# Products without a reader in TensorE's gaps, a new order for the first batch, and rows turned by DMA, in a cross-attention and quantised FFN kernel

## The chip, the core and the metric

The kernel runs on one core of one Trainium2 chip. The metric is the device time of one execution in microseconds; the kernel before was executed three times, and one further execution was recorded by the hardware profiler. All times below come from that recording and those runs. TensorE works at one of two clocks, 1.2 or 2.4 GHz; the profile gives the granted clock as a share of the higher one.

## The reference

Eight batches of 512 x 512 rows in float32. First an attention whose keys and values are the same context, then a feed-forward layer whose inputs, weights and hidden block are rounded to 8-bit steps:

```python
# x, context: (8, 512, 512); mask: (8, 512, 512) bool, True is masked
q = layernorm(x)
s = where(mask, -1e9, einsum('bqd,bkd->bqk', q, context) / sqrt(512))
att = einsum('bqk,bkd->bqd', softmax(s), context)
x = x + einsum('bdl,ol->bdo', swapaxes(att, -1, -2), W_merge) + b_merge

xq = fake_quant(layernorm(x), clip_x)      # one scale: the largest |value| of all batches
g  = xq @ weight_quant(w_gate).T           # w_gate, w_up: (1408, 512)
u  = xq @ weight_quant(w_up).T
h  = fake_quant(silu(g) * u, clip_down)    # again one scale for all batches
x  = x + h @ weight_quant(w_down).T        # w_down: (512, 1408)
```

Both scales need a maximum over all batches. So the kernel has three parts, one after the other: attention for all batches, gate and up for all batches, down for all batches.

## The kernel before

**Attention** (`attention`, from line 86). A batch of 512 rows is T = 4 tiles of 128. Products are made in three float32 pieces: each operand is split into a high part (copied by ScalarE) and a low part (subtracted by VectorE), and `product` (L744) adds hi·hi, hi·lo and lo·hi, over four steps of contraction twelve matmuls of 128x512 into one PSUM bank. For a batch, TensorE turns the context (turns g = 0 to 3, four 128x128 transposes each) and the normalised rows (turns g = 4 to 7) by `transposes` (L726) into the banks `tr[g % 4]`; ScalarE copies the high part out (`transposed_hi`, L367) and VectorE subtracts the low part (`transposed_lo`, L480). Then come the scores (`scores`, banks mm0 to mm3), the mask and row maximum on VectorE (`mask_and_max`, L527), the exponential on ScalarE, the sum's inverse, `probs_hi` and `probs_lo` (L544), the products with W_merge (`mixed`, L769), and those with the context (`merged`, L762), to which VectorE adds the residual. The order of work is written out by hand for each engine; the engines meet only by semaphores. From the second batch on the products of batch n - 1, the turns of batch n + 1 and the scores of batch n are woven together.

The first batch has an order of its own. Its rows and its context come in four DMAs each; SP issues row tile 0, context tiles 0 to 3, row tiles 1 to 3, the mask, W_merge, and then the loads of the next batch (L261 to L273). TensorE turns the four context tiles and then, for k = 0 to 3, row tile k, scores(0,k), and a quarter of W_merge (`merge_transpose`, L776, into `tr[k]`). VectorE takes the row statistics of tile t (`first_norm`, L493), POOL raises the variance to the power -1/2 (`make_rstd1`, L319), VectorE makes the bias (`first_bias`, L502). Only when all four tiles are through does POOL turn the mask into a summand, in one piece of 128x2048 (`make_mneg`, L313). VectorE then goes through the tiles one at a time: mask and maximum, a low part of W_merge (`merge_lo`, L487), the inverse, and `probs_lo` of the same tile, which waits for ScalarE's exponential and `probs_hi`. The turns of batch 1's context wait for the low parts of W_merge, since they share banks; `mixed(0, 0)` waits for all of them (L773).

SP also stores the finished rows, and turns the quantised weights by DMA transposes (`turn_w`, L238: L242 turns a tile of 128x512 float16, L246 one of 128x1408).

At its end attention leaves two last steps to VectorE and POOL: the variances of the last batch's rows, and the largest distance from the mean.

**Gate and up** (`ffn`, from line 813). The largest value of all rows is found by a turn on TensorE (L1181), a reduction, a second turn (L1183) and a few small operations of VectorE. Then the rows of batch 0 are scaled and rounded to int8 (`layer_norm` on ScalarE, L979, half of batch 0 by VectorE, L1087), cast to float16 integers `xi` (`quantise`, L1057), turned by TensorE in 16 transposes of 128x128 (`turn`, L1153, banks tp0 and tp1), and copied out to `xT` (`take_xT`, L985, and L1093). A step is one batch: for each of NI = 11 tiles `gate_up` (L1168) makes four matmuls for gate and four for up, ScalarE takes silu (L996), VectorE multiplies (L1074) and keeps the largest (L1082). The next batch is scaled at i = 0 of the step, cast at i = 2 and 3, turned by TensorE behind i = 6 and copied out by ScalarE behind i = 8:

```python
                    def step(b, p):
                        for i in range(NI):
                            gate_up(b, p, i)
                            if i == 6 and not static(b, B - 1):
                                turn(b + 1, 1 - p)
```

Five hidden blocks stay in SBUF; the first three of the eight are stored to DRAM by SP (L932, 2.8 MB each) after their step, and SP loads the rows of batch n + 2 (L920) when those of batch n have been scaled.

**Down.** The maximum over all hidden values is found by POOL (L963). ScalarE rounds each hidden block in four pieces (L1022), VectorE casts them (`widen_hidden`, L1118), and TensorE makes 44 matmuls per batch (`down`, L1194, L1210); VectorE scales and adds the residual, SP stores.

## Time and profile before

| | |
|---|---|
| three runs | 579.19, 579.25, 579.32 us; median 579.25 |
| the profiled execution | 579.35 us, its span 577.6 us |
| TensorE | 543.1 us busy, 94% of the span, 2610 matmuls; mean granted clock 0.976 |
| VectorE, ScalarE, POOL | 454.3, 296.1 and 148.8 us busy |
| DMA | 82.59 MB, 143 GB/s over the span; 306 GB/s in the first of 40 slices |
| attention, first batch to the products with W_merge | 0 to 41.6 us |
| attention, to its last product | 41.6 to 318.7 us |
| from there to gate/up's first product | 318.7 to 329.8 us |
| gate and up, eight steps | 329.8 to 490.5 us |
| from there to down's first product | 490.5 to 495.5 us |
| down, to its last product | 495.5 to 573.1 us |

A line of the profile names the line of the kernel, the engine, the operation, and what it writes and reads; a duration is that of one instruction as recorded. Matmuls are pipelined, so the recorded durations overlap, and the pace is the distance between starts. In `ffn` several names share one tile: `xi`, `xT` and silu's results appear as `hid`, the float16 hidden block as `gu_T`, and four of the output banks as `gu`, two as `tp`.

### The profile page before, as it was taken

What the parts mean: (1) busy time and instruction counts of PE and PEld (TensorE: products, weight loads), DVE (VectorE), ACT (ScalarE), POOL (GpSimd) and SP (SyncE); (2) the same over time, 40 slices, a digit from 0 to 9 for tenths busy, and PEclk for the clock granted to TensorE, in tenths of its full rate; (3) what the DMA queues carried; (4) which work ended last, traced back from release to release, by engine and by line L of the source; (5) the groups of instructions that cost most, each with busy time, mean ns of one, the idle gap of its engine ahead of it and who ended that gap; (6) DMA issues with size and microseconds to landing.
All of it is one profiled execution on the core that took longest, in us unless ns stands there. A gap on an engine that the chain in (4) does not pass through costs nothing. (4 is left out here: it accounts for less than half of the span.)

```text
span 577.6 us, 7625 instructions
## 1 busy us (share of the span) xinstructions
PE 543.1 (94%) x2610; PEld 359.9 (62%) x2610; DVE 454.3 (79%) x839; ACT 296.1 (51%) x431; POOL 148.8 (26%) x77
## 2 busy tenths in 40 slices
PE   6759999999999999999999499999999999699996
PEld 4547888888888888888888244444444444244442
DVE  5279889887988988889686557878777877599884
ACT  3356465545645556355431357556645743777520
POOL 1707454636545365463421000000000000000000
PEclk9969999999999999999999699999999999899999
DMA  8520535454354443441229513272060000779783
GB/s 306 184 74 1 133 136 183 136 189 88 119 174 128 170 124 121 165 134 74 48 112 150 186 73 170 104 273 73 12 260 0 0 0 2 269 269 396 244 288 153
DMA packets 47583, 82.59 MB, mean 143 GB/s; under 512 B 20416, under 2 KB 24512, under 8 KB 44992
## 3 DMA queue, kind: packets, MB, share of 16 engines
q1 hardware_dynamic: 47552, 82.20, 42.8%
q8 instruction: 17, 0.28, 0.2%
q14 instruction: 14, 0.11, 0.1%
HBM read 52.43 MB, written 25.43 MB: 135 GB/s over the span
## 5 line engine op out<-in xcount | busy, mean ns | idle before, releaser
L1176 PE MATMUL gu<-hid,gu_T 128*128 128x512 f16 x704 | 155.6, 383 | 0.8 <-DVE hid L1093 0.8
L1176 PEld LDWEIGHTS gu<-hid,gu_T 128*128 128x128 f16 x704 | 68.9, 99 | 84.1 <-issue 3.3
L1074 DVE SCALAR_TENSOR_TENSOR hid<-gu,gu_mul,hid 128x512 f32 (+1 forms) x88 | 65.2, 747 | 41.0 <-PE gu L1176 35.7
L996 ACT ACTIVATE hid<-gu,gu_mul 128x512 f32<-128x512 f32 x88 | 59.8, 686 | 70.4 <-PE gu L1176 64.9
L1210 PE MATMUL gu<-wd_T,gu_T 128*128 128x512 f16 x264 | 59.1, 385 | 5.0 <-DVE gu_T L1118 5.0
L546 DVE SCALAR_TENSOR_TENSOR p_lo<-probs,rinv,p_hi 128x512 fp32r<-128x512 f32 x32 | 39.8, 1243 | 21.4 <-ACT p_hi L386 21.0
L750 PE MATMUL mm<-cT_hi,qT_hi 128*128 128x512 f32 x128 | 51.2, 400 | 5.6 <-DVE qT_lo L484 5.6
L1022 ACT ACTIVATE h<-hid,inv 128x512 int8<-128x512 f32 (+3 forms) x32 | 44.2, 1456 | 17.9 <-DVE gu_T L1118 14.1
L1082 DVE TENSOR_REDUCE hmax<-hid 128x1 f32 (+2 forms) x48 | 53.1, 1119 | 0.0
L750 PE MATMUL mm<-wm_hi,p_hi 128*128 128x512 f32 x128 | 53.0, 414 | 0.0
L379 ACT ACTIVATE probs<-probs,nmax 128x512 f32<-128x512 f32 x32 | 23.2, 724 | 56.7 <-DVE nmax L537 56.7
L750 PE MATMUL mm<-g_hi,c_hi 128*128 128x512 f32 x128 | 52.2, 408 | 0.0
L344 POOL TENSOR_TENSOR c_lo<-cx,c_hi 128x2048 fp32r<-128x2048 f32 x8 | 37.0, 4626 | 54.3 <-ACT c_hi L414 54.2
L752 PE MATMUL mm<-wm_hi,p_lo 128*128 128x512 f32 x128 | 50.7, 396 | 0.0
L752 PE MATMUL mm<-cT_hi,qT_lo 128*128 128x512 f32 x128 | 50.4, 394 | 0.0
L751 PE MATMUL mm<-wm_lo,p_hi 128*128 128x512 f32 x128 | 50.4, 394 | 0.0
L751 PE MATMUL mm<-cT_lo,qT_hi 128*128 128x512 f32 x128 | 50.4, 394 | 0.0
L752 PE MATMUL mm<-g_hi,c_lo 128*128 128x512 f32 x128 | 50.2, 393 | 0.0
L751 PE MATMUL mm<-g_lo,c_hi 128*128 128x512 f32 x128 | 49.9, 390 | 0.0
L1210 PEld LDWEIGHTS gu<-wd_T,gu_T 128*128 128x128 f16 x264 | 26.0, 99 | 37.5 <-DVE gu_T L1118 5.8
L963 POOL PARTITION_ALL_REDUCE top<-hmax x1 | 0.4, 380 | 171.2 <-DVE hmax L1106 171.2
L393 ACT ACTIVATE g_hi<-mm 128x512 fp32r<-128x512 f32 x32 | 19.0, 597 | 48.5 <-PE mm L752 48.5
(123 smaller groups left out, 958.6 us busy)
## 6 DMA issues: line engine op xcount, KB each, us to landing
h_dram<-hid SPq DMA_DIRECT2D x3, 2816.0 KB, 12.9
hid<-h_dram SPq DMA_DIRECT2D x3, 2816.0 KB, 14.0
cx<-in_ctx_dram SPq DMA_DIRECT2D x7, 1024.0 KB, 7.5
x<-in_x_dram SPq DMA_DIRECT2D x5, 1024.0 KB, 5.3
x_dram<-x SPq DMA_DIRECT2D x20, 256.0 KB, 2.4
xq<-x_dram SPq DMA_DIRECT2D x5, 1024.0 KB, 5.9
x<-x_dram SPq DMA_DIRECT2D x5, 1024.0 KB, 6.4
hid<-x_dram SPq DMA_DIRECT2D x4, 1024.0 KB, 6.5
```

The lines of the kernel that those rows point to most:

```text
L344: nc.gpsimd.tensor_tensor(c_lo[:], cx[n % 2][:], c_hi[:].bitcast(F32), ALU.subtract).then_inc(c_ready, 1)
L379: nc.scalar.activation(probs[t % 3][:], probs[t % 3][:], ACT.Exp, bias=nmax[:, t:t + 1], scale=SCALE, accum_out=rsum[:, t:t + 1]).then_inc ...
L546: nc.vector.scalar_tensor_tensor(p_lo[:, t, :], probs[t % 3][:], rinv[:, t:t + 1], p_hi[:, t, :].bitcast(F32), ALU.mult, ALU.subtract).the ...
L750: nc.tensor.matmul(bank[:], a_hi[:, t, cols], b_hi[:, t, :], start=t == 0, stop=False)
L751: nc.tensor.matmul(bank[:], a_hi[:, t, cols], b_lo[:, t, :], start=False, stop=False)
L752: last = nc.tensor.matmul(bank[:], a_lo[:, t, cols], b_hi[:, t, :], start=False, stop=t == T - 1)
L996: nc.scalar.activation(silu[SILU_AT[i]], gu[2 * (i % 3)][:], ACT.Silu, scale=gu_mul[:, 0, i:i + 1]).then_inc(silu_done, 1)
L1022: nc.scalar.activation(h8[:, a:b, :].rearrange("p i l -> p (i l)"), hid[:, slot2(s), a * L:b * L], ACT.Copy, scale=inv[:, 1:2]).then_inc(h ...
L1074: nc.vector.scalar_tensor_tensor(hid[:, b % SLOTS, i * L:(i + 1) * L], gu[2 * (i % 3) + 1][:], gu_mul[:, 1, i:i + 1], silu[SILU_AT[i]], AL ...
L1082: nc.vector.tensor_reduce(hmax[:, k:k + 1], hid[:, b % SLOTS, lo * L:hi * L], AX_X, ALU.max, apply_absolute_value=True).then_inc(hmaxed, 1)
L1176: last = nc.tensor.matmul(gu[2 * (i % 3) + g][:], gu_T[:, g, h, i * P:(i + 1) * P], xT[p][:, h, :], start=h == 0, stop=h == T - 1)
L1210: last = nc.tensor.matmul(yb[T * (s % 2) + t][:], hq[s % 2][:, i, t * P:(t + 1) * P], wd_T[:, i, :], start=i == 0, stop=i == NI - 1)
```

## The change

It has four parts.

1. *First batch.* TensorE's order of turns becomes context 0, rows 0, context 1, 2, 3 (`FIRST_TURNS`); the turns of row tiles 1 to 3 stand in the middle of scores(0,0), (0,1) and (0,2), and go to banks mm1, mm2, mm3 and tr0. The quarters of W_merge follow scores(0,0), (0,1) and, two together, (0,2), in banks tr1, tr2, tr3, tr1. Row tiles 2 and 3 share their statistics, their rstd and their bias. POOL makes the mask's summand in four pieces, the first ahead of the last rstd. VectorE makes `probs_lo` of tile t - 1 behind the mask of tile t; the row statistics of batch 1 come before its context's subtractions.
2. *Rows turned by DMA.* For batches 1 to 7 SP issues four DMA transposes from `xi` to `xT`; TensorE's turns, ScalarE's copies and their waits go. SP's order in a step becomes: load of the batch after next, wait for the casts, four transposes, then (batches 1 to 3) wait for the maximum and store of the hidden block of the batch before.
3. *Products without a reader.* 13 behind attention's last product, 11 ahead of the turns of batch 0, 4 behind them, and 20 between up and down.
4. Waits and counts of semaphores follow.

```diff
+                FIRST_TURNS = (0, T, 1, 2, 3, T + 1, T + 2, T + 3)
+                def turns(n, g):
+                    return 2 * T * n + (FIRST_TURNS.index(g) if n == 0 else g) + 1
+                def turn_bank(n, g):
+                    if n == 0 and T <= g < 2 * T - 1:
+                        return mm[g - T + 1]
+                    return tr[0] if n == 0 and g == 2 * T - 1 else tr[g % 4]
+                FIRST_ROWS = ((0, 1), (1, 2), (2, T))
+                def merge_bank(k):
+                    return tr[1 + k % 3]
...
# POOL
-                    make_rstd1(0)
-                    make_mneg(0)
+                    first_rstd(0)
+                    first_rstd(1)
+                    first_mneg(0)
+                    first_rstd(2)
+                    for t in range(1, T):
+                        first_mneg(t)
...
# ScalarE
-                    for g in range(T + 1):
+                    for g in FIRST_TURNS[:T + 1]:
                         transposed_hi(0, g)
                     norm1(0, 1)
+                    transposed_hi(0, T + 1)
                     norm1(0, 2)
-                    transposed_hi(0, T + 1)
                     norm1(0, 3)
-                    transposed_hi(0, T + 2)
...
                             exps(n, t)
                             if start:
-                                if t == 0:
-                                    transposed_hi(0, 2 * T - 1)
+                                if t < 2:
+                                    transposed_hi(0, T + 2 + t)
                                 probs_hi(n, t)
-                                merge_hi(t)
+                                for k in ((0,), (1,), (2, 3), ())[t]:
+                                    merge_hi(k)
...
# VectorE
-                    first_norm(0)
+                    first_stats(0)
                     first_bias(0)
...
-                    for g in range(T + 1):
+                    transposed_lo(0, 0)
+                    transposed_lo(0, T)
+                    first_stats(1)
+                    for g in (1, 2, 3):
                         transposed_lo(0, g)
-                    for t in range(1, T):
-                        first_norm(t)
-                        first_bias(t)
-                        if t > 1:
-                            transposed_lo(0, T + t - 1)
+                    first_bias(1)
+                    first_stats(2)
+                    first_bias(2)
+                    transposed_lo(0, T + 1)
...
                             if start:
-                                if t == 0:
-                                    transposed_lo(0, 2 * T - 1)
-                                else:
-                                    merge_lo(t - 1)
+                                if t:
+                                    probs_lo(n, t - 1)
+                                    for k in ((0,), (1,), (2, 3))[t - 1]:
+                                        merge_lo(k)
                                 invert_sum(n, t)
-                                probs_lo(n, t)
+                                if t < 2:
+                                    transposed_lo(0, T + 2 + t)
...
                         if start:
-                            merge_lo(T - 1)
-                            for k in range(T):
+                            probs_lo(n, T - 1)
+                            row_stats1(n + 1, 0, T)
+                            transposed_lo(n + 1, 0)
+                            row_bias1(n + 1)
+                            for k in range(1, T):
                                 transposed_lo(n + 1, k)
-                            row_stats1(n + 1, 0, T)
-                            row_bias1(n + 1)
...
# TensorE
                         for t in range(T):
+                            if turn is not None and t == T // 2:
+                                transposes(0, turn)
...
                     pe.wait_ge(consts, 4)
-                    for g in range(T):
+                    for g in FIRST_TURNS[:T + 1]:
                         transposes(0, g)
                     for n in range(B):
                         last, start = n == B - 1, n == 0
                         for k in range(T):
-                            if start:
-                                transposes(0, T + k)
                             scores(n, k)
                             if start:
-                                merge_transpose(k)
+                                for g in ((0,), (1,), (2, 3), ())[k]:
+                                    merge_transpose(g)
...
                     for k in range(T):
                         merged(B - 1, k)
+                    for _ in range(13):
+                        nc.tensor.matmul(tr[0][:], c_hi[:, 0, 0:P], g_hi[:, 0, :], start=True, stop=True)
...
# gate and up: SP
-                    for b in range(SPILL):
-                        for n in (2 * b, 2 * b + 1):
-                            sp.wait_ge(affine, T * (n + 1))
-                            if n == 0:
-                                sp.wait_ge(own_affine, T // 2)
+                    sp.wait_ge(affine, T)
+                    sp.wait_ge(own_affine, T // 2)
+                    load(2, 0, x_in)
+                    for n in range(1, B):
+                        sp.wait_ge(affine, T * (n + 1))
+                        if n + 2 < B:
                             load(n + 2, n % 2, x_in)
-                        sp.wait_ge(hrun, b + 1)
-                        sp.dma_start(h_dram[b], hid[:, b, :]).then_inc(slot_free, 16)
-                        sp.wait_ge(slot_free, 16 * (SLOTS + b + 1))
+                        sp.wait_ge(ints, 2 * (n + 1))
+                        for t in range(T):
+                            sp.dma_start_transpose(xT[n % 2][:, :, t * P:(t + 1) * P], xi[:, t, :]).then_inc(xT_in[n % 2], 16)
+                        if n <= SPILL:
+                            sp.wait_ge(hrun, n)
+                            if n > 1:
+                                sp.wait_ge(slot_free, 16 * (SLOTS + n - 1))
+                            sp.dma_start(h_dram[n - 1], hid[:, n - 1, :]).then_inc(slot_free, 16)
...
# gate and up: ScalarE, VectorE, TensorE
-                            if i == 8 and not last:
-                                take_xT(b + 1, 1 - p)
...
-                        if not static(b, 0):
-                            dve.wait_ge(turned, 2 * b)
+                        if static(b, 1):
+                            dve.wait_ge(turned, 2)
+                        elif not static(b, 0):
+                            dve.wait_ge(xT_in[1 - p], times(b, 2 - p, 64) - 64 * p)
...
                         if i == 0:
-                            pe.wait_ge(xT_out, 2 * (b + 1))
+                            if static(b, 0):
+                                pe.wait_ge(xT_out, 2)
+                            else:
+                                pe.wait_ge(xT_in[p], times(b, p, 64) - 64 * (1 - p))
...
+                    def keep_busy(products, bank):
+                        for _ in range(products):
+                            nc.tensor.matmul(bank[:], wd_T[:, 0, 0:P], wd_T[:, 1, :], start=True, stop=True)
...
+                    keep_busy(11, gu[5])
                     turn(0, 0)
+                    keep_busy(4, gu[5])
                     def step(b, p):
                         for i in range(NI):
                             gate_up(b, p, i)
-                            if i == 6 and not static(b, B - 1):
-                                turn(b + 1, 1 - p)
...
+                    keep_busy(20, tp[0])
                     for s in range(B):
                         down(s)
```

## Rows read from the trace of the kernel before

**Rows 1.** Waits of TensorE over the span: us in total, times, longest.
```profile
PE tr L740 <- DVE wm_lo L490: 6.6, 3, 2.8
PE mm L750 <- DVE qT_lo L484: 5.6, 4, 1.4
PE gu L1210 <- DVE gu_T L1118: 5.0, 1, 5.0
PE tp L1181 <- DVE tops L1042: 4.3, 1, 4.3
PE tp L1163 <- DVE hid L1067: 2.7, 1, 2.7
```

**Rows 2.** Timeline of TensorE, first batch: start us, us, line, operation, idle before.
```profile
4.14 4.00 PE L740 MATMUL tr<-ident,cx 128*128 128x128 f32 x16 [4.14 <-DMA cx<-in_ctx_dram]
...
10.41 0.80 PE L750 MATMUL mm<-cT_hi,qT_hi 128*128 128x512 f32 x1 [1.41 <-DVE qT_lo L484]
...
22.58 0.50 PE L750 MATMUL mm<-cT_hi,qT_hi 128*128 128x512 f32 x1 [1.41 <-DVE qT_lo L484]
...
25.45 0.60 PE L781 MATMUL tr<-ident,x 128*128 128x128 f32 x4
25.88 0.60 PE L740 MATMUL tr<-ident,qn 128*128 128x128 f32 x4
...
41.60 0.77 PE L750 MATMUL mm<-wm_hi,p_hi 128*128 128x512 f32 x1
```

**Rows 3.** Timelines of VectorE and POOL, first batch.
```profile
5.32 0.55 DVE L644 TENSOR_SCALAR qn<-xq,rstd,nmr 128x512 f32<-128x512 f32 x1
...
18.92 5.41 POOL L317 TENSOR_SCALAR mneg<-mk 128x2048 bf16<-128x2048 uint8 x1
...
29.88 0.68 DVE L533 CUSTOM_DVE_ANT_0 probs<-mm,mneg 128x512 f32<-128x512 f32 x1
...
32.59 0.75 DVE L546 SCALAR_TENSOR_TENSOR p_lo<-probs,rinv,p_hi 128x512 fp32r<-128x512 f32 x1 [0.79 <-ACT p_hi L386]
```

**Rows 4.** Busy time and granted clock in short windows (clock: third number from the end).
```profile
320.80:321.00 0.20, 0.00 (x0) 0.00 (x0) 0.17 (x3) 0.00 (x0) 0.00 (x0) 0.76 0.96 369
...
334.40:334.60 0.20, 0.20 (x2) 0.12 (x1) 0.00 (x0) 0.20 (x2) 0.00 (x0) 0.60 0.00 0
```

**Rows 5.** The chain that ended last, gate and up: start us, us, what.
```profile
326.96 2.07 PE tp L1163 x16
...
329.81 14.59 PE gu L1176 x56
...
345.29 18.99 PE gu L1176 x88
364.28 0.89 PE tp L1163 x16
```

**Rows 6.** DMA issues of the page: count, KB each, median us to landing.
```profile
h_dram<-hid SPq DMA_DIRECT2D x3, 2816.0 KB, 12.9
...
d_scale_dram<-d_step SPq DMA_DIRECT2D x4, 0.5 KB, 11.1
```

**Rows 7.** Line L242, DMA transposes of weights: ns of one issue, us to landing.
```profile
L242 SPq DMA_TRANSPOSE gu_T<-wst x22: 1195/1267/2092, 63.7 to 284.4; - x22
...
DMA to landing us min/median/max: 2.4/2.5/3.9
```

**Rows 8.** Window with four such transposes (DMA share: second number from the end).
```profile
208.20:213.30 5.10, 5.10 (x26) 4.23 (x25) 4.88 (x14) 2.95 (x7) 3.00 (x3) 1.00 0.50 101
```

**Rows 9.** Timelines of SP and VectorE, the step that begins at 352.2.
```profile
355.00 0.32 SPq L932 DMA_DIRECT2D h_dram<-hid  x1
...
360.35 0.69 DVE L1067 CAST hid<-y 128x1024 f16<-128x1024 int8 x1
```

**Rows 10.** Chain and timeline at the start of down.
```profile
495.47 15.85 PE gu L1210 x66
...
496.02 0.69 DVE L1118 CAST gu_T<-h 128x1024 f16<-128x1024 int8 x1 [0.61 <-ACT h L1022]
```

More of the change, by code:

```diff
@@ L368, in transposed_hi @@
                     def transposed_hi(n, g):
-                        act.wait_ge(t_done, 2 * T * n + g + 1)
+                        act.wait_ge(t_done, turns(n, g))
                         if n and g in (0, T):
@@ L736, in transposes, with product @@
                             pe.wait_ge(q_ready, T * n + g - T + 1)
-                            pe.wait_ge(t_lo, 2 * T * n + g - T + 1)
+                            if n:
+                                pe.wait_ge(t_lo, turns(n, g - T))
+                            elif g == 2 * T - 1:
+                                pe.wait_ge(t_lo, turns(n, 0))
                             src = qn
                         for h in range(T):
-                            last = nc.tensor.transpose(tr[g % 4][:, h * P:(h + 1) * P],
+                            last = nc.tensor.transpose(turn_bank(n, g)[:, h * P:(h + 1) * P],
                                                        src[:, g % T, h * P:(h + 1) * P], ident[:])
                         last.then_inc(t_done, 1)
-                    def product(bank, a_hi, a_lo, b_hi, b_lo, m, done, split=None, before=0):
+                    def product(bank, a_hi, a_lo, b_hi, b_lo, m, done, split=None, before=0, turn=None):
                         cols = slice(m * P, (m + 1) * P)
                         for t in range(T):
+                            if turn is not None and t == T // 2:
+                                transposes(0, turn)
                             if m == 0 and split is not None:
@@ L758, in scores @@
                             pe.wait_ge(g_ready, T * (n - 1) + k + 1)
-                        pe.wait_ge(t_lo, 2 * T * n + T + k + 1)
-                        product(mm[k], qT_hi, qT_lo, cT_hi, cT_lo, k, s_done)
+                        pe.wait_ge(t_lo, max(turns(n, T + k), turns(n, T - 1)))
+                        product(mm[k], qT_hi, qT_lo, cT_hi, cT_lo, k, s_done,
+                                turn=T + k + 1 if n == 0 and k < T - 1 else None)
                     def merged(m, k):
@@ L984, in take_xT @@
                     def take_xT(b, p):
-                        for g in range(1 if static(b, 0) else 2):
-                            act.wait_ge(turned, 2 * b + g + 1)
-                            nc.scalar.activation(xT[p][:, 2 * g:2 * g + 2, :].rearrange("p h l -> p (h l)"),
-                                                 tp[g][:].bitcast(F16), ACT.Copy).then_inc(xT_out, 1)
+                        act.wait_ge(turned, 1)
+                        nc.scalar.activation(xT[p][:, 0:2, :].rearrange("p h l -> p (h l)"),
+                                             tp[0][:].bitcast(F16), ACT.Copy).then_inc(xT_out, 1)
                     def take_gate(b, i):
```

79 lines of the change are left out of this document (43 added, 36 removed).

## The prediction

> **What bounds the kernel now.** I read the waits of TensorE first, then the timeline of the first batch, the granted clock in short windows, the chain that ended last, and the DMA issues. Outside a few places TensorE is never idle, so each microsecond of its work or waiting is a microsecond of the kernel, and its waits are the list of what can be had [rows 1]: 6.6 us for the low parts of W_merge and 5.6 us (four times 1.4) for turned rows, both in the first batch; 4.3 and 2.7 us between attention and gate/up; 5.0 us between up and down. A further loss is no wait: in the longer of them the granted clock falls from 2.4 to 1.2 GHz and is back only after some microseconds of work [rows 4]. It fell at 320.9, about 2.2 us after attention's last product, and came back at 334.5, 4.7 us after gate/up's first one. The products with W_merge also began at the low clock (the first took 0.77 us, where one at 22.58 took 0.50), while the gaps of 1.4 us before them had cost none [rows 1, 2].
>
> **First batch.** Two things are to be seen: scores(0,0), begun at 10.41, is long done when POOL multiplies its mask, in one piece from 18.92 to 24.33, behind the last row's rstd; and after it tile follows tile on VectorE and ScalarE at 3.4 us each (mask at 29.88, p_lo's end at 33.34), while TensorE waits [rows 2, 3]. The products with W_merge begin at 41.60 [rows 2], and from there to attention's end TensorE doesn't wait. So the gain is by how much that start moves. Step by step:
> - Turns now run context 0, rows 0, context 1, 2, 3. Row 0 is normalised by 5.87 [rows 3]; its turn and the three behind it at 1.0 us each (sixteen matmuls in 4.00 [rows 2]) end at 10.0, copy and subtraction take the 1.4 of the wait for turned rows: scores(0,0) starts at 11.4 where it was 10.41. **Worse by 1.0.**
> - Its twelve products with a turn of four between them: if the clock rises in their midst, as it did, 4.3 us, to 15.7; if the slightly less dense work before keeps the clock low 3 us longer, to 17.4.
> - Then TensorE has three products of twelve at 2.87 and six turns of four at 0.43 [rows 2], 11.2 in one piece, for rows' turns stand inside the products: scores(0,3) ends at 26.5 to 28.2, where it was 30.8 (the turn at 25.88, 2.0 for turn, copy and subtraction, 2.9 for the products). Cover: mask row 0 is ready at some 11.5 (2.3 MB are in the queue up to its end, 7.5 us at the first slice's 306 GB/s; a quarter of 5.41 is 1.35), rows 1 to 3 by 18; a tile's work on VectorE is what it was, 3.4 us with its waits for ScalarE inside, just under TensorE's 3.7.
> - After the last score comes one tile's chain, 3.46 us (mask at 29.88 to p_lo's end at 33.34 [rows 3]), with two subtractions for W within it, and TensorE waits 2.5 us for those, then turns three context rows in 1.3: the products with W_merge begin at 30.8 to 32.5, and at the low clock at first, as they did before (where the turns are slow too, the clock is back that much earlier in the products). The gain is **9.0 to 10.8**; I take **9.5**, nearer the low end, since TensorE's work ahead of the scores is thinner than it was.
> The second batch's row statistics now come before its context's subtractions on VectorE, so its norm is ready earlier against that start than it was: no new wait. POOL's order (mask, then c_lo) shifts with it.
>
> **Turns of batches 1 to 7.** On TensorE these are 16 f16 transposes, 0.89 us a batch, between steps of 18.99 [rows 5]: seven are **6.2 us** of pure path, and with them go two copies of ScalarE, which isn't the bound. In their place SP issues four DMA transposes a batch at 1.27 us each [rows 7], 5.1 us, and the last lands 2.5 us behind its issue [rows 7]. The integers are ready 8.9 us into a step (the second cast ends at 361.0, the step began at 352.2: 345.29 and 32 of 88 products) [rows 5, 9]. So without other traffic they land at 8.9 + 3.8 + 2.5 = 15.2 of 19.0: 3.8 us of cover. In three steps the 2.8 MB store of the hidden block goes out 2.8 us into the step (355.00), and the load of the next batch behind it; the queue keeps its order (a store of 0.5 KB took 11.1 us to land behind 2 MB of loads [rows 6]). The store lands by 2.8 + 12.9 = 15.7; the four transposes hold the DMA engines half busy for 5.1 us [rows 8], 2.6 us of their time, so they land at 18.3 to 19.0, or at 21 if they run behind the store at their issue pace: 0 to 2 us late in each of three steps. I take 0.3 a step, being nearer the queue's own share, so **1.0 lost of 6.2**. SP's later work in such a step (the wait for the maximum, the store) is due 8 us after its last transpose is issued, so nobody waits behind SP. Transposing by TensorE here is cheap; first the rows: 0.89 us for 16 at 2.4 GHz and 2.07 at 1.2 GHz [rows 5].
> The Trainium skill (TensorE: Matmul & The Clock Gate, Part 4: PE-mode transpose) gives about 275 ns for one in a kernel's context and says that the full clock doesn't engage for it; by that the seven turns would be 30.8 us, an estimate from that page, and the gain some 25 us more. The trace disagrees, with 56 ns each at the full clock, so that case gets no chance.
>
> **Attention to gate/up.** Thirteen products at 0.24 us (twelve took 2.87 [rows 2]) follow attention's last one, from 318.6 to 321.7. TensorE waited 4.3 us there, until 323.0, for VectorE's largest distance, so they delay nothing while 1.3 us of that are left. Then the two small turns as before, then eleven products at 0.216 in the wait of 2.7 that ends with the integers at 326.96 [rows 1, 5]: from 324.25 to 326.6. If the clock holds, the 16 turns take 0.89 instead of 2.07, the copy 0.78 as before, and the four products behind the turns end 0.1 after it: gate/up starts at 328.7, not 329.81. Its first 56 products took 14.59, 12.08 at the later pace: 2.5 lost to the clock [rows 5]. Gain 1.1 + 2.5 = **3.6**. What is left is 2.6 us with two small turns in it, the longest idle piece 1.3: as a piece no longer than the gaps of 1.4 that cost no clock, in all a little longer than the 2.2 after which it fell [rows 4]. If it falls, eleven products take 4.7 and hold up the turns by some 2, but it returns earlier: 0.4 to 2.6 of gain, 1.6 likely.
>
> **Up to down.** Twenty products, 4.3 us of the 5.0 idle, leave 0.6. The first 66 products of down took 15.85, where 66 at the pace of gate/up take 14.24: 1.6 lost to the clock [rows 10]. At the full clock four products take 0.86 and then wait for the second cast, whose end is 496.71, 0.4 us; 0.2 more at the last piece. **1.0 gained**; 0.9 to 1.6.
>
> **Sum.** 9.5 + 5.2 + 3.6 + 1.0 = 19.3 us. The profiled execution took 579.35 for a span of 577.6, 0.1 over the median of the three runs (579.25), so 579.35 - 19.3 - 0.1 = **560.0 us**.
>
> **Rivals.**
> - *The clock falls between attention and gate/up all the same.* For it: 2.6 us with only two tiny matmuls. Against: the longest idle piece is 1.3. Gain there 1.6: **562**. Chance 0.22.
> - *Transposes late by their full bound behind the stores.* Three steps of 2 us: 5 us more than in the sum, **565**. For it: 3.8 MB in the queue ahead. Against: the engines' own share is 2.6 us. Chance 0.12.
> - *The first batch's gain is given back*, because another engine bounds the second one (VectorE is busy for most of it): 5 of 9.5 stay hidden, **565**. Against: TensorE had no wait at all there. Chance 0.08.
> - *Slower: DMA transposes late in every step.* If a batch's four land one after another at the 3.9 us that the slowest needed [rows 7], they end at 8.9 + 15.6 = 24.5, 5.5 late, in seven steps 38.5: 579.3 - 20.3 + 38.5 = **597**. It decides from 2.9 us late a step. Against it: attention's transposes were issued 1.27 us apart and each landed 2.5 us on. Chance 0.04.
> - *The products without a reader don't hold the clock anywhere and the first batch's chain stays as it is*: only the turns go, and 2 us of lateness in three steps eats that: 579. Chance 0.02.
> The Trainium skill (DMA: Bandwidth & Descriptors, Queues, rings and completion order) says that each DMA engine takes descriptors in ring order; the 11.1 us for 0.5 KB agrees, and the second rival is that rule carried to its end.
>
> **How the numbers follow.** The forecast has 0.52, with a range of its own of 558 to 561.5. Low end: 10.8 + 6.2 + 3.6 + 1.6 = 22.2 would give 557.0, so 556.5; high end takes in the first three rivals and two of them together: 567. A measurement of this kernel tells about 0.2% (1.2 us) from no change. Faster by more 0.94, within it 0.02, slower 0.04.
>
> **What would show it.** In the changed profile: products with W_merge starting at 31 to 33 us; mask rows on POOL by 18; no idle time of TensorE in the steps between batches, or a wait on transposes in exactly the three steps with a store; steps 19.0 us apart; granted clock full from 322 on and gate/up's first 56 products in 12.1; the first 66 of down in some 14.9. The forecast is wrong if TensorE waits in the second batch, or if a step without a store waits for a transpose.

## The result, and the profile after

The changed kernel takes **558.56 us** (median of four runs, 557.97 to 560.10), the kernel before 579.22 beside it (578.79 to 579.32): a ratio of 0.9649, 95% interval 0.9628 to 0.9669. The forecast was 560.0 in a range of 556.5 to 567.0. The profiled execution is the slowest of the four, 560.10 us for a span of 558.3, so the sum has to be held against 579.35 - 560.10 = 19.25 us; the other 1.5 us of the median's 20.7 is scatter between executions, of which more below.

The page of the changed kernel, busy time, and from the waits of TensorE (line, what was waited for: us in total, times, longest):

```profile
PE 541.5 (97%) x2546; PEld 357.5 (64%) x2546; DVE 451.3 (81%) x837; ACT 283.5 (51%) x417; POOL 149.8 (27%) x79
```

```profile
PE tr L776 <- DVE wm_lo L515: 2.5, 1, 2.5
PE mm L788 <- DVE cT_lo L509: 2.0, 1, 2.0
PE tp L1236 <- DVE tops L1089: 1.3, 1, 1.3
PE gu L1265 <- DVE gu_T L1167: 0.9, 2, 0.6
```

Against [rows 1]: the 6.6 us for the low parts of W_merge are 2.5, the four waits for turned rows are gone (one of 2.0 for turned context stands in their place, ahead of scores(0,0)), 4.3 before gate/up is 1.3, 2.7 is gone, 5.0 before down is 0.9. No wait for a turned row of batches 1 to 7 is in the list. A shorter wait is not yet a gain, though: in two of these places TensorE now runs products instead of waiting. What counts is when the next useful product starts.

**First batch.** The timeline of TensorE (start, us, line, operation, idle before):

```profile
11.59 0.80 PE L788 MATMUL mm<-cT_hi,qT_hi 128*128 128x512 f32 x1 [2.03 <-DVE cT_lo L509]
...
14.77 0.48 PE L788 MATMUL mm<-cT_hi,qT_hi 128*128 128x512 f32 x1
...
27.20 0.60 PE L776 MATMUL tr<-ident,cx 128*128 128x128 f32 x4
30.29 1.59 PE L776 MATMUL tr<-ident,cx 128*128 128x128 f32 x12 [2.50 <-DVE wm_lo L515]
31.55 0.76 PE L788 MATMUL mm<-wm_hi,p_hi 128*128 128x512 f32 x1
```

and those of POOL and VectorE:

```profile
11.12 1.54 POOL L338 TENSOR_SCALAR mneg<-mk 128x512 bf16<-128x512 uint8 x1 [0.73 <-DMA mk<-in_mask_BxSxS_bk_dram]
...
14.28 4.64 POOL L338 TENSOR_SCALAR mneg<-mk 128x512 bf16<-128x512 uint8 x3
```

```profile
16.44 0.69 DVE L562 CUSTOM_DVE_ANT_0 probs<-mm,mneg 128x512 f32<-128x512 f32 x1
...
27.40 0.69 DVE L562 CUSTOM_DVE_ANT_0 probs<-mm,mneg 128x512 f32<-128x512 f32 x1 [0.34 <-PE mm L790]
```

The products with W_merge start at 31.55 instead of 41.60 [rows 2], and attention's last product at 308.24 instead of 318.34: all **10.1 us** arrive. Between 11.59 and 27.20, where the last product of scores(0,3) ends, TensorE doesn't wait once. VectorE's four maskings now follow at 3.65 us (16.44 to 27.40), TensorE's own pace for a tile, and the last of them waits for TensorE, not the other way round.

**Attention to gate/up, and up to down.** Timelines of TensorE:

```profile
308.24 0.39 PE L790 MATMUL mm<-g_hi,c_lo 128*128 128x512 f32 x1
308.46 3.11 PE L854 MATMUL tr<-g_hi,c_hi 128*128 128x512 f32 x13
312.88 0.27 PE L1236 MATMUL tp<-ident,tops 128*1 128x128 f32 x1 [1.32 <-DVE tops L1089]
313.77 0.22 PE L1238 MATMUL tp<-ident,top_row 1*128 1x1 f32 x1 [0.62 <-DVE top_row L1094]
313.92 3.98 PE L1233 MATMUL gu<-wd_T 128*128 128x512 f16 x11
317.69 1.35 PE L1210 MATMUL tp<-ident,hid 128*128 128x128 f16 x16
...
476.91 1.04 PE L1265 MATMUL gu<-wd_T,gu_T 128*128 128x512 f16 x4 [0.64 <-DVE gu_T L1167]
```

The granted clock in windows of 1 us (third number from the end), and the chain that ended last:

```profile
314.00:315.00 1.00, 1.00 (x5) 0.42 (x6) 0.83 (x5) 0.00 (x0) 0.00 (x0) 0.94 0.54 213
315.00:316.00 1.00, 1.00 (x4) 0.32 (x3) 0.97 (x3) 1.00 (x2) 0.00 (x0) 0.50 1.04 442
...
318.00:319.00 1.00, 1.00 (x17) 0.98 (x15) 0.00 (x0) 0.37 (x1) 0.00 (x0) 0.85 0.74 295
```

```profile
319.90 152.06 PE gu L1226 x704
...
492.04 4.75 PE tp L1265 x22
```

From attention's last product to gate/up's first it is 11.59 us (308.24 to 319.83), where it was 11.47 [rows 5]: nothing gained. The clock fell from 2.4 to 1.2 GHz at 314.9, one microsecond after the eleven products had begun, so these took 3.98 and the turns began 1.0 us after they might have (experiment 5 shows the integers ready 8.5 us after attention's last product; that is 316.7 here, and the turns start at 317.69). But it is back at 318.3, so that gate/up starts at the full clock, and all 704 products of eight batches take 152.06 without a gap: the 2.5 us that gate/up lost before are the whole gain, less 0.1, **2.4 us**. Down's first 88 products take 19.88 (476.91 to 496.79) instead of 20.60, **0.7 us**.

**Turned rows.** TensorE's seven turns are gone: **6.2 us**. SP's transposes in the step that begins at 357.8 (duration ns, first and last start; then us to landing), behind the store of 2.8 MB:

```profile
L978 SPq DMA_TRANSPOSE hid<-hid x4: 1339/1629/3103, 366.5 to 371.2; - x4
...
DMA to landing us min/median/max: 5.4/6.9/8.7
```

The last of them lands at 371.2 + 5.4 = 376.6; the step that reads it begins at 319.90 + 3 × 18.99 = 376.9. Nobody waits, with some 0.3 us to spare; in the other two steps with a store it is 0.7 and 1.8 us. The sum 10.1 + 2.4 + 0.7 + 6.2 = 19.4 agrees with the 19.3 by which the span fell (577.6 to 558.3).

### The profile page after: what moved, and what is told of

Its sections match the earlier page's. It is cut to its first block and busy times, and to the rows that moved or that the text cites. A ratio compares the mean times of both kernels' runs of the same rounds, so it can differ in the third digit from the quotient of the medians.

```text
span 558.3 us, 7480 instructions
## 1 busy us (share of the span) xinstructions
PE 541.5 (97%) x2546; PEld 357.5 (64%) x2546; DVE 451.3 (81%) x837; ACT 283.5 (51%) x417; POOL 149.8 (27%) x79
## 5 line engine op out<-in xcount | busy, mean ns | idle before, releaser
L1226 PE MATMUL gu<-hid,gu_T 128*128 128x512 f16 x704 | 152.1, 379 | 0.0
L575 DVE SCALAR_TENSOR_TENSOR p_lo<-probs,rinv,p_hi 128x512 fp32r<-128x512 f32 x32 | 41.2, 1286 | 19.1 <-ACT p_hi L411 18.8
L1069 ACT ACTIVATE h<-hid,inv 128x512 int8<-128x512 f32 (+3 forms) x32 | 44.2, 1456 | 17.2 <-DVE gu_T L1167 13.4
## 6 DMA issues: line engine op xcount, KB each, us to landing
hid<-h_dram SPq DMA_DIRECT2D x3, 2816.0 KB, 12.9
```

The costliest lines, as they stand in the source:

```text
L575: nc.vector.scalar_tensor_tensor(p_lo[:, t, :], probs[t % 3][:], rinv[:, t:t + 1], p_hi[:, t, :].bitcast(F32), ALU.mult, ALU.subtract).the ...
L1069: nc.scalar.activation(h8[:, a:b, :].rearrange("p i l -> p (i l)"), hid[:, slot2(s), a * L:b * L], ACT.Copy, scale=inv[:, 1:2]).then_inc(h ...
L1226: last = nc.tensor.matmul(gu[2 * (i % 3) + g][:], gu_T[:, g, h, i * P:(i + 1) * P], xT[p][:, h, :], start=h == 0, stop=h == T - 1)
```

## The experiments

Every ratio is against the kernel before in the same session, with its 95% interval. The first four ran together (before: 580.09 us), then four (580.71), then four (580.21).

### 1. The first batch's order of before, all else changed

```diff
-                    for g in FIRST_TURNS[:T + 1]:
+                    for g in range(T):
                         transposes(0, g)
...
                         for k in range(T):
+                            if start:
+                                transposes(0, T + k)
                             scores(n, k)
...
-                    first_rstd(0)
-                    first_rstd(1)
-                    first_mneg(0)
-                    first_rstd(2)
-                    for t in range(1, T):
-                        first_mneg(t)
+                    make_rstd1(0)
+                    make_mneg(0)
```

> Everything of the change except the first batch's order, which is the one of the kernel before. By the trace of the changed kernel the products with W_merge started 10.1 us earlier (31.55 for 41.60) and attention's last product also 10.1 us earlier (308.24 for 318.34), so if TensorE's order alone sets the rest this should take 558.6 + 10 = 568.6 us (567.5 to 569.7). Rival (part of the gain belongs to something else, since the parts overlap): below 566.

Measured: 569.61 us, 0.9827 [0.9799, 0.9855]. TensorE's list of waits opens as in [rows 1], and the first product with W_merge is at 40.13:

```profile
PE tr L740 <- DVE wm_lo L490: 7.0, 3, 2.8
PE mm L750 <- DVE qT_lo L484: 6.2, 4, 1.8
```

Beside the kernel of experiment 4, which ran in the same session and differs from the changed one in twenty products alone (558.96), it is 10.6 us, and up to 1.3 more, since that kernel lacks the twenty: the first batch's order carries what the timeline says, and none of it is given back later. By the traces alone the two starts of W_merge lie 8.6 apart (40.13 and 31.55). In this execution scores(0,0) began at the full clock (0.50 for its first product, 0.80 in the changed kernel's), as it did in that of experiment 4, where W_merge starts at 29.95, 10.2 earlier.

### 2. Turns of batches 1 to 7 on TensorE, all else changed

```diff
                             gate_up(b, p, i)
+                            if i == 6 and not static(b, B - 1):
+                                turn(b + 1, 1 - p)
...
-                        for t in range(T):
-                            sp.dma_start_transpose(xT[n % 2][:, :, t * P:(t + 1) * P], xi[:, t, :]).then_inc(xT_in[n % 2], 16)
```

> Everything of the change except the DMA transposes: the turns of batches 1 to 7 are TensorE's again. If the DMA transposes are wholly hidden, seven turns of 0.89 us come back: 558.6 + 6.2 = 564.8 us (564 to 565.8). Rival of the prediction, transposes late by some tenths behind the stores: 563.8 or less, and waits of TensorE at the starts of steps 2 to 4 in the changed kernel's trace, which it doesn't show.

Measured: 564.41 us, 0.9715 [0.9689, 0.9741], 5.4 us over experiment 4 (up to 6.7 with the twenty products counted as there). The chain that ended last shows the turns between steps:

```profile
330.83 0.89 PE tp L1206 x16
331.72 18.99 PE gu L1219 x88
```

Sixteen f16 transposes take 0.89 us in a stretch at the full clock, 56 ns each. The Trainium skill (TensorE: Matmul & The Clock Gate, Part 4: PE-mode transpose) has some 275 ns for a bf16 one in a kernel's context and the full clock not engaging for them; here too the rows disagree, and moving 112 of them to the DMA queue is worth 5 to 7 us, not the 31 that the page's figure would make of them by estimate.

### 3. No products between attention and gate/up

```diff
-                    for _ in range(13):
-                        nc.tensor.matmul(tr[0][:], c_hi[:, 0, 0:P], g_hi[:, 0, :], start=True, stop=True)
...
-                    keep_busy(11, gu[5])
                     turn(0, 0)
-                    keep_busy(4, gu[5])
```

> The 13 + 11 + 4 products without a reader between attention and gate/up are left out. Theory A (the clock): gate/up starts some 11.5 us behind attention's last product and its first 56 products lose 2.5 us to the low clock: 558.6 + 2.4 = 561.0 us; up to 3.6 more than the changed kernel in executions where that one's clock never fell. Rival B (the products don't matter, the rest of the change moves the clock): within 0.5 us of 558.6.

Measured: 562.20 us, 0.9684 [0.9664, 0.9705], 3.2 us over experiment 4. From its chain:

```profile
317.73 2.08 PE tp L1207 x16
...
320.58 154.08 PE gu L1223 x704
```

The turns are back at the low clock (2.08 us), and the 704 products of gate/up take 154.08, 2.0 more than 152.06. From attention's last product to gate/up's first it is 11.36 us, so by the traces the products bring 1.8 us against the changed kernel's profiled execution and 2.7 against that of experiment 5. The 3.2 by time holds more than that: here the clock rose only at 17.0 in the first batch, and the products with W_merge started at 33.92.

### 4. No products between up and down

```diff
-                    keep_busy(20, tp[0])
```

> The 20 products between up and down are left out. The changed kernel's first 88 products of down took 19.88 us, the one before 20.60: with the low clock back 558.6 + 0.7 = 559.3 us. Rival: the pieces of the hidden block arrive too late for the clock to matter, no difference, 558.6 us.

Measured: 558.96 us, 0.9634 [0.9609, 0.9659]: by its time it can't be told from the changed kernel. Its trace can, in the chain:

```profile
473.84 16.46 PE gu L1265 x66
490.31 4.75 PE tp L1265 x22
```

The first 88 products take 21.2 us (16.46 and 4.75), against 19.88 with the twenty and 20.60 in the kernel before. So the twenty bring 0.7 us against the kernel before, and 1.3 against the changed kernel without them, no more than the scatter between executions. The differences to this experiment that are given above are too small by up to these 1.3.

### 5. The changed kernel again

No edit; it stands beside the next three.

> The changed kernel once more, beside the next three on one chip: 558.6 us, with executions between 558 and 560.1 as before, since the clock falls between attention and gate/up in some of them (gate/up's start costs 1.2 us more then) and holds in others.

Measured: 557.96 us (557.83 to 558.70), 0.9611 [0.9577, 0.9645]. In this execution (557.83 us) the same code kept its clock between attention and gate/up. Windows and timeline:

```profile
314.00:315.00 1.00, 1.00 (x5) 0.29 (x3) 0.97 (x3) 1.00 (x2) 0.00 (x0) 1.00 1.02 434
```

```profile
306.84 0.39 PE L790 MATMUL mm<-g_hi,c_lo 128*128 128x512 f32 x1
...
312.53 2.55 PE L1233 MATMUL gu<-wd_T 128*128 128x512 f16 x11
...
317.55 2.76 PE L1226 MATMUL gu<-hid,gu_T 128*128 128x512 f16 x12
```

The idle times of 1.3 and 0.6 us are those of the other execution, to 0.01; the eleven products take 2.55, not 3.98, and the middle 10.71, not 11.59. Its products with W_merge start at 31.58 as the other's do, but at the full clock (0.47 us the first, not 0.76). The first difference is 0.9 us; by the second, attention ends 1.4 us earlier (306.84, not 308.24). Together they are the 2.3 us that lie between the two profiled executions (560.10 and 557.83).

### 6. Each transpose issued twice

Four more transposes go out ahead of the four real ones, into an unused place, and the waits count both. Nothing of the computation is left out.

```diff
                         for t in range(T):
+                            sp.dma_start_transpose(spare_xT[:, :, t * P:(t + 1) * P], xi[:, t, :]).then_inc(xT_in[n % 2], 16)
+                        for t in range(T):
                             sp.dma_start_transpose(xT[n % 2][:, :, t * P:(t + 1) * P], xi[:, t, :]).then_inc(xT_in[n % 2], 16)
```

> SP issues eight DMA transposes a batch, four into an unused place first and then the four that count, and TensorE waits for all. Theory (the transposes have some 3.8 us of cover without a store and about 1.5 with one): the last lands at 9 + 7 x 1.27 + 2.5 = 20.4 of 19.0 us in the four steps without a store, 1.4 late, and at 9 + 13 + 2.5 = 24.5 in the three with a store, where four already took 7.1 to 7.8 us to issue: 5 late. 558.6 + 6 + 15 = 579 us (568 to 582). Rival: the cover is much larger than reckoned: below 562.

Measured: 574.72 us, 0.9894 [0.9852, 0.9935]. TensorE's wait, and the chain through the first step:

```profile
PE gu L1229 <- DMA hid<-hid: 11.8, 7, 2.7
```

```profile
326.44 1.21 SPq L979
...
335.54 2.50 DMA hid<-hid
...
338.18 1.91 PE gu L1229 x8
...
465.51 20.87 PE gu L1229 x88
```

The chain now runs through SP's queue: seven issues at 1.3 us, and the eighth lands 2.5 us after its start, at 338.04. The step's integers were ready at 326.44, so four would have landed at 332.8, four microseconds ahead of the next step. With eight the landing is 20.2 us into the step (20.4 was expected), where the step's own work takes 19.0. Behind a store it is 359.74 - 338.18 = 21.6, where 24.5 was expected: there the issues took 1.2 to 2.0 us each and the last landed in 2.5. All seven steps wait, 11.8 us in all, and the time rises by 16.8 over experiment 5. Of the rest 3.4 us are clock: behind the two longest waits (2.5 us at 359.87 and 2.7 us at 465.51) a step's 88 products took 20.9 us, and behind the other five (1.1 to 1.6 us) 19.2. The three steps with a store waited 2.5, 1.3 and 1.6 us, hardly longer than the four others, where 5 us each had been expected. What the experiment settles is how the price of transposes is made: issues in a row, then one landing.

### 7. The first mask in one piece, behind the rows' rstd

```diff
-                    first_mneg(0)
                     first_rstd(2)
-                    for t in range(1, T):
-                        first_mneg(t)
+                    first_mneg()
```

> The first batch's mask is multiplied in one piece again, behind the last rstd, all else as changed. Theory (the mask's readiness holds the first batch): it ends at 14.28 + 5.41 = 19.7 us, and the first mask step of VectorE, which began at 16.44, moves by 3.3: 558.6 + 3.3 = 561.9 us. Rival (TensorE's order alone made the gain): 558.6 to 559.5.

Measured: 561.30 us, 0.9674 [0.9637, 0.9711], 3.3 us over experiment 5. From VectorE's timeline:

```profile
19.42 0.69 DVE L559 CUSTOM_DVE_ANT_0 probs<-mm,mneg 128x512 f32<-128x512 f32 x1 [3.17 <-POOL mneg L337]
...
29.58 0.69 DVE L559 CUSTOM_DVE_ANT_0 probs<-mm,mneg 128x512 f32<-128x512 f32 x1 [1.42 <-PE mm L787]
```

and from TensorE's:

```profile
22.42 0.50 PE L785 MATMUL mm<-cT_hi,qT_hi 128*128 128x512 f32 x1 [2.04 <-DVE qT_lo L506]
```

The first masking waits 3.2 us for POOL, and the subtraction for turned rows 2, which stands behind it on VectorE, comes late for scores(0,2): TensorE waits 2.0 us, once. So the last masking, which waits for TensorE again, is 2.2 us late, and the products with W_merge start at 33.73 instead of 31.58. The other 0.9 of the 3.1 us between the two profiled executions is the clock, which fell ahead of gate/up here (11.60 us from attention's last product to gate/up's first) and held in experiment 5 (10.71).

### 8. The kernel before, with its first mask in four pieces

The same cut made alone, on the kernel before.

```diff
-                    make_mneg(0)
+                    gp.wait_ge(mask_in, 16)
+                    for t in range(T):
+                        nc.gpsimd.tensor_scalar(mneg[:, t, :], mk[:, t, :], MASKED, None, ALU.mult).then_inc(mneg_made, 1)
```

> The kernel before, with one edit: the first batch's mask is multiplied in four pieces, each waited for by its own tile. Theory (the mask matters only together with the order of VectorE, where mask 0 stands behind the low part of rows 2, done at 22.5): mask 0 begins at 22.5 instead of 24.49, 2.0 us gained, a ratio to the kernel before of 0.9965. Rival (the mask alone was the loss): it begins as soon as its piece is there, 20.3 or earlier, and 4 us or more are gained, a ratio of 0.993 or less.

Measured: 579.67 us, 0.9994 [0.9972, 1.0015]: **no gain** that can be told, where the theory expected 2.0 us and the rival 4. The products with W_merge start at 42.08, where they were at 41.60. In this execution the clock fell to 1.2 GHz in scores(0,1), from 17.0 to 20.4 us, and the turn of rows 3 is at 26.87, not at 25.88 [rows 2]: 1.0 us late for a reason that isn't the mask, so that 0.5 us at most came from the mask. From VectorE's and TensorE's timelines:

```profile
23.44 0.68 DVE L535 CUSTOM_DVE_ANT_0 probs<-mm,mneg 128x512 f32<-128x512 f32 x1
...
28.14 0.69 DVE L486 TENSOR_TENSOR qT_lo<-tr,qT_hi 128x512 fp32r<-128x512 f32 x1 [3.82 <-ACT qT_hi L376]
```

```profile
26.87 0.60 PE L742 MATMUL tr<-ident,qn 128*128 128x128 f32 x4
```

The mask of tile 0 is applied early, and then VectorE idles 3.8 us: its next instruction subtracts the high part of turned rows 3, which TensorE turns only at 26.87, after scores(0,2), and the rest of tile 0 is queued behind it. So the late mask was not alone in holding the old chain: the rows turned between the scores held it about as late. With experiment 7: of the 10 us, the mask's pieces are worth 2.1 where the turns are in the new order, and within 0.5 nothing where they are not. How the other 8 divide between the order of turns, that of the row statistics and that of `probs_lo` was not tried.

### 9 and 10. Only the thirteen, or only the eleven

```diff
-                    keep_busy(11, gu[5])
                     turn(0, 0)
-                    keep_busy(4, gu[5])
```

> Of the products between attention and gate/up only the 13 behind attention stay. Theory (both groups are needed, since what is left idle is then 5 us, from 311.4 on, against 2.2 us at which the clock fell before): as without any, +2 to +3 us over the changed kernel. Rival (the first group alone holds the clock): +0.5 or less.

Measured: 561.71 us (560.63 to 562.79), 0.9678 [0.9645, 0.9712].

```diff
-                    for _ in range(13):
-                        nc.tensor.matmul(tr[0][:], c_hi[:, 0, 0:P], g_hi[:, 0, :], start=True, stop=True)
```

> Of the products between attention and gate/up only the 11 and 4 around the turns stay. Theory: the clock falls in the 4.3 us behind attention, the 11 products take 4.7 us instead of 2.4 and hold the turns up by some 1.2, but the clock is back when gate/up starts: +0 to +1.2 us over the changed kernel, since some of its own executions have just this. Rival (they only delay): +3 us.

Measured: 558.92 us (558.52 to 559.16), 0.9636 [0.9608, 0.9664]. The chains of the two, thirteen only first:

```profile
316.49 2.08 PE tp L1210 x16
...
319.34 154.97 PE gu L1226 x704
```

```profile
312.73 3.81 PE gu L1230 x11
316.54 0.89 PE tp L1207 x16
...
318.30 152.06 PE gu L1223 x704
```

The thirteen alone change nothing against no products at all: the clock falls, and gate/up's 704 products take 154.97. The eleven alone run at the low clock for most of their 3.8 us, but bring it back before the turns (0.89 us) and gate/up. Between the two lie 2.8 us, without overlap of their runs. Both came as the theories had it.

### 11 and 12. Every gap filled

The theory that was left says that each idle place of more than a microsecond may cost clock. So: small f16 products ahead of the first turns and the first scores, ten products in the wait of 2.5 us for W_merge, 15 for 13 after attention, three more in the two small waits behind them, and the cast ahead of down in five pieces.

```diff
                     pe.wait_ge(consts, 4)
+                    small(16)
                     for g in FIRST_TURNS[:T + 1]:
                         transposes(0, g)
+                        if g == 0:
+                            small(6)
+                    small(18)
...
+                            if start and k == 0:
+                                pe.wait_ge(masked, 1)
+                                for _ in range(10):
+                                    nc.tensor.matmul(mm[0][:], wm_hi[:, 0, 0:P], wm_hi[:, 0, :], start=True, stop=True)
...
-                    for _ in range(13):
+                    for _ in range(15):
...
-            PIECES = ((0, 1), (1, 3), (3, 6), (6, NI))
+            PIECES = ((0, 1), (1, 2), (2, 4), (4, 7), (7, NI))
...
+                    keep_busy(1, gu[5])
                     pe.wait_ge(top_made, 1)
...
+                    keep_busy(2, gu[5])
                     pe.wait_ge(top_spread, 1)
```

> An attempt to be faster than both: small products without a reader from 2.1 us on and ahead of scores(0,0), ten in the wait for W's low parts, 15 instead of 13 behind attention, one and two around the small turns, and the hidden block rounded in five pieces (1, 1, 2, 3, 4 tiles) instead of four. By the low clock's losses: up to 1.5 at the start, 1.9 at the products with W_merge (3.7 us at half rate), 1.2 before gate/up, 0.7 at down: 558.6 - 4.5 = 554 us (553 to 557). Rival (the clock's rise and fall don't follow such products, or they delay the chain): 558 to 560.

Measured: **556.05 us** (555.93 to 556.09), 0.9574 [0.9540, 0.9607], 1.9 us under experiment 5 beside it and faster than both kernels. In the profiled executions 1.5 of the 1.8 us between this kernel and experiment 5 lie ahead of W_merge. The last experiment has 12 and 3 small products for 16 and 6:

```diff
-                    small(16)
+                    small(12)
...
-                            small(6)
+                            small(3)
```

> The kernel with all gaps filled, with fewer small products at the start (12 and 3 for 16 and 6), so that the first turns aren't held up: in the filled one turn 0 started 0.37 us and the rows' turn 0.28 us later than in the changed kernel. Expected 0.2 to 0.4 us less than the filled one's ratio of 0.9574 to the kernel before, if the clock rises as early; if it doesn't, 0.5 to 1 us more.

Measured: 556.01 us (555.90 to 556.18), 0.9585 [0.9557, 0.9613], the same; the 0.2 to 0.4 us expected of it did not come. The timeline of the first of them:

```profile
9.08 1.17 PE L828 MATMUL mm<-ident 128*128 128x128 f16 x18
11.49 0.50 PE L788 MATMUL mm<-cT_hi,qT_hi 128*128 128x512 f32 x1 [1.25 <-DVE cT_lo L509]
...
26.11 2.57 PE L850 MATMUL mm<-wm_hi 128*128 128x512 f32 x10
...
30.10 0.48 PE L788 MATMUL mm<-wm_hi,p_hi 128*128 128x512 f32 x1
```

Scores(0,0) starts no earlier (11.49), but at 2.4 GHz: 0.50 us for its first product, where it was 0.80. From there on every product runs at the full clock; the products with W_merge start at 30.10, attention to gate/up takes 10.70, and down's first 88 products 19.6 (19.88 in the changed kernel). Four runs lie within 0.16 us of one another, where those of the changed kernel lie within 0.87 in the same session. (The fast start can come without the small products: experiment 4's profiled execution has 0.50 too, and W_merge at 29.95.)

## Why the prediction was right

By its steps, with what was measured beside each (us):

| step | forecast | profiled execution | where shown |
|---|---|---|---|
| first batch | 9.5 (9.0 to 10.8) | 10.1 | timeline; undone: 10.6 by time |
| turns, without lateness | 6.2 | 6.2 | undone: 5.4 by time |
| transposes late behind stores | -1.0 | 0 | no wait |
| attention to gate/up | 3.6 | 2.4 (3.3 in experiment 5) | undone: 3.2 by time |
| up to down | 1.0 | 0.7 | undone: 1.3 by trace |
| sum | 19.3 | 19.4 | |

**First batch: right, step by step.** Scores(0,0) was set at 11.4 and came at 11.59; the clock rose in its midst, at 14.7; the last product of scores(0,3) ended by 27.2 (26.5 to 28.2); W_merge began at 31.55 (30.8 to 32.5). Mask row 0 was ready at 12.7, 1.2 later than forecast, and the last at 18.9 (18); no engine waited for either. What the prediction had wrong is the reason it gave first. It laid the chain to the mask, "in one piece from 18.92 to 24.33". Experiment 8 took that away and gained nothing that can be told: VectorE's queue held the same tile about as long for turned rows 3. The number came out because the sum followed the new order engine by engine and did not rest on that reason.

**Turns: the gain right, its cost too high.** The prediction took 1.0 us for lateness in the three steps with a store. The measured landing, 18.8 us into the step, lies inside the forecast's 18.3 to 19.0, yet 0.3 us before the end of the step, and the other two came earlier, at 18.3 and 17.2: a landing that is just in time costs nothing, and a mean over a range that ends at the deadline was the wrong way to price it. Two mistakes stood against each other there: the store landed in 9.3 us, not 12.9 (that is the median of three in the kernel before; the store of [rows 9] itself landed in 8.5), but the transposes behind it were issued at up to 3.1 us each instead of 1.27, and landed after up to 8.7 instead of 2.5. The Trainium skill (DMA: Bandwidth & Descriptors, Queues, rings and completion order) has each DMA engine take its descriptors in ring order, and this fits: the first of four transposes took 7.1 to 8.7 us and landed 0.5 us behind the load of the next batch, which had gone out behind the store and landed in 10.7 to 12.2, and the last took 3.9 to 5.4. It is that load which held them, 15.3 to 16.9 us into the step; the prediction names it but has no time for it in the sum. By experiment 6, 5.2 us more of SP's queue a step would have turned the gain of 6 us over TensorE's turns into a loss of 10 (0.9894 against 0.9715).

**Attention to gate/up: half right.** The prediction held that the clock stays up because no idle piece is over 1.3 us, and gave 0.22 to the rival in which it falls all the same. In the profiled execution it fell, at 314.9; in experiment 5, with the same idle times, it held. Of the seven profiled executions that have all 28 products it fell in four (11.5 to 11.6 us from attention's last product to gate/up's first) and held in three (10.7). So "as a piece no longer than the gaps of 1.4 that cost no clock" is the step that failed: the length of a piece doesn't decide it by itself. The rival's price (1.6) was too low too, because the clock was back before gate/up. The prediction set all fifteen products together; experiments 9 and 10 show that the thirteen alone bring nothing and that the eleven and four carry the gain, since they raise the clock again ahead of gate/up where it has fallen. Where the clock holds as in experiment 5, the gain is 3.3 of the 3.6 forecast.

**Up to down:** 0.7 of 1.0, by the same mechanism; the total can't tell it, the trace can.

The rival with seven late steps (597 us) needed 3.9 us to land for each transpose in turn; in the steps without a store each landed in 2.5 and overlapped the next issue, as in [rows 7]. Experiment 6 is the nearest thing to that rival, and has its sign. The second batch gave nothing back.

## What to carry to other kernels

When a chain of waits has two holders that end at about the same time, removing the one in sight gains nothing; follow the queue of the engine that is released and ask what its *next* instruction waits for. Products without a reader are worth their place where they end just before dense work begins, since they pay the slow start in time that was idle anyway; filled completely, such gaps also make the time repeatable. Moving 0.9 us from TensorE to a DMA queue that needs 6.4 us for it pays only while the deadline is farther off than the whole queue, stores ahead of it included: read the landing of the worst step against the start of the next.

## What the runs showed of the hardware that was not expected

- **The moment at which the granted clock moves is not fixed to the work.** With idle times equal to 0.01 us it fell in one execution and held in the next; in the first batch, the first products with W_merge took 0.76 in one and 0.47 in the other. Of nine profiled executions with the new first batch and no small products, two began scores(0,0) at the full clock (experiments 2 and 4), and in experiment 3 it rose only at 17.0; the products with W_merge started at 29.95 in experiment 4 and at 33.92 in experiment 3. That spreads the runs of the changed kernel over 2.3 us in all (557.83 to 560.10) and those of the kernel before over 4.8 (577.89 to 582.67); with the gaps filled, 8 runs on two chips lie between 555.90 and 556.18. A gain of one microsecond in such a kernel is better read from the trace than from the times.
- **Small products count as work, as far as the runs show.** With 22 (or 15) f16 products of 128x128 among the first turns, the eighteen behind those took 1.17 us, 65 ns each, so the clock was at 2.4 GHz from 9.1 (9.4) us on, in both profiled executions. With the transposes alone seven of nine began scores(0,0) at the low clock, until 14.7 in the changed kernel's. That it is the small products which make the difference rests on these few traces and on the close times of the eight runs.
- **SP's own queue stretches behind a store.** A DMA transpose that SP issues in 1.27 us took up to 3.10 behind 2.8 MB of store and 1 MB of load, so that even the issuing engine was held.
